# Hard attention in a four-layer graph kernel: a finished tile is added to X by ScalarE and GpSimd instead of VectorE

## What is computed

```python
attn = jnp.einsum('hqd,hkd->hqk', Q, K) * SCALING + energy
attn = attn + jnp.where(adj > 0, 0.0, -jnp.inf)
attn = jax.nn.softmax(attn, axis=-1)
hard = (attn == jnp.max(attn, axis=-1, keepdims=True)).astype(jnp.float32) / HEADS
out = jnp.einsum('hqk,hkd->hqd', hard, V)
return out.transpose(1, 0, 2).reshape(n, EMBED)
...
x = x + _L2_gnn_ref(h, adj, ...)
```

## Time and profile before

| what | value |
|---|---|
| median of 3 runs | 2402.12 us (2400.92 to 2402.3) |
| the profiled execution: its time / its span | 2401.43 / 2399.7 us |
| DVE busy, share of the span | 1979.6 us, 82% |
| PE busy / PEld busy | 2103.3 / 1713.7 us |
| ACT busy / POOL busy | 1768.2 / 694.6 us |
| hard attention, first DVE chunk to last X addition | 1331.0 to 2162.1 us |
| granted TensorE clock, mean | 0.949 of full speed |

### The profile page before, as it was taken

How to read it: one execution, slowest core, us unless ns; L and a number is a source line. 1 busy time by engine, 2 the same in 40 slices (tenths; PEclk the granted TensorE clock), 3 DMA queues, 4 the chain that set the end, 5 groups by cost and what they waited for, 6 DMA issues and landing times. The chain is left out here.

```text
span 2399.7 us, 62590 instructions
## 1 busy us (share of the span) xinstructions
PE 2103.3 (88%) x25316; PEld 1713.7 (71%) x25316; DVE 1979.6 (82%) x4384; ACT 1768.2 (74%) x2206; POOL 694.6 (29%) x646
## 2 busy tenths in 40 slices
PE   4647999999957999999978798999998999884999
PEld 3537999999944888888855466666666666554888
DVE  5566999999985988888867799999999999995122
ACT  4546999999975877777754688888888988884000
POOL 0020000000000000000003677778777877860000
PEclk9958999999978999999979799999999999996999
DMA  9787212212102011101007211111111111202222
GB/s 298 278 322 300 91 62 72 81 60 88 58 5 71 22 43 43 43 22 43 23 14 171 93 65 65 66 65 65 65 65 52 50 62 65 65 5 77 71 75 68
DMA packets 78474, 201.08 MB, mean 84 GB/s; under 512 B 26897, under 2 KB 44491, under 8 KB 74745
## 3 DMA queue, kind: packets, MB, share of 16 engines
q1 hardware_dynamic: 77432, 197.27, 24.5%
q10 hardware_dynamic: 768, 0.00, 0.0%
HBM read 161.87 MB, written 26.86 MB: 79 GB/s over the span
## 5 line engine op out<-in xcount | busy, mean ns | idle before, releaser
L1614 DVE CUSTOM_DVE_ANT_0 h_S<-h_ps,h_off 128x832 f32<-128x832 f32 x832 | 800.4, 1019 | 13.9 <-POOL h_off L1476 10.8
L1521 PE MATMUL h_ps<-KS,h_QS 98*128 98x416 f16 x1664 | 442.2, 348 | 99.9 <-DVE h_mx L1614 65.6
L1581 ACT ACTIVATE h_H<-h_S,h_nmx 128x2048 fp8e4<-128x2048 f32 x208 | 416.6, 2003 | 110.5 <-DVE h_nmx L1620 110.5
L834 ACT ACTIVATE b_CA<-b_el,HC 128x1152 fp8e4<-128x1152 f32 (+1 forms) x384 | 435.4, 1219 | 3.2 <-DMA b_el<-el_dram 3.2
L931 PE MATMUL b_pb<-b_x,b_B 128*128 128x132 f16 x5408 | 414.2, 221 | 3.9 <-DVE b_B L896 3.4
L931 PEld LDWEIGHTS b_pb<-b_x,b_B 128*128 128x128 fp8e4 x5408 | 340.3, 96 | 6.6 <-DVE b_B L896 6.2
L1482 POOL TENSOR_SCALAR h_gap<-h_S,h_nmx 128x1280 f32<-128x1280 f32 x208 | 277.1, 1332 | 145.0 <-DVE h_nmx L1620 142.5
L912 PE MATMUL b_pz<-b_x,adjT 128*128 128x134 f16 x2704 | 256.5, 221 | 15.8 <-DMA b_x<-xv_dram 15.8
L1487 POOL TENSOR_SCALAR h_H<-h_gap 128x1280 uint8<-128x1280 f32 x208 | 260.5, 1252 | 17.1
L1552 PEld LDWEIGHTS h_po<-Vhl,h_HT 128*128 128x128 fp8e4 x5408 | 214.8, 98 | 65.0 <-ACT h_HT L1588 0.7
L1245 PE MATMUL c_pd<-c_mv,WnT 128*128 128x256 f16 x2028 | 250.9, 275 | 10.8 <-DMA c_ad<-adjT_dram 10.8
(11 more groups left out here) (208 smaller groups left out, 3300.5 us busy)
## 6 DMA issues: line engine op xcount, KB each, us to landing
h_rows<-in_adj_dram SPq DMA_DIRECT2D x25, 1663.5 KB, 7.7
b_x<-xv_dram SPq DMA_DIRECT2D x48, 435.5 KB, 5.2
s_rows<-in_adj_dram SPq DMA_DIRECT2D x25, 832.0 KB, 6.7
s_rows<-in_adj_dram SPq DMA_DIRECT2D x25, 831.5 KB, 8.1
adjT_dram<-adjT SPq DMA_DIRECT2D x1, 10816.0 KB, 38.0
c_ad<-adjT_dram SPq DMA_DIRECT2D x13, 832.0 KB, 6.1
m_ad<-adjT_dram SPq DMA_DIRECT2D x13, 832.0 KB, 4.5
b_el<-el_dram SPq DMA_DIRECT2D x16, 576.0 KB, 3.8
```

The costliest lines, as they stand in the source:

```text
L834: nc.scalar.activation(dst[:, 0:cols], elr[:, n % 2, 0:cols], ACT.Sigmoid, bias=HC[:, h, 1, jt:jt + 1], scale=STEP, saturate=False).then_i ...
L1521: last = nc.tensor.matmul(ps[:, ch % 2, b, 0:SB], QS[:, i % 2, h, :], KS[:, h, c0:c0 + SB], start=True, stop=True)
L1581: nc.scalar.activation(H[:, g % 2, 0:CA], S[:, g % 2, 0:CA], ACT.Exp, bias=nmx[:, g % 2:g % 2 + 1], scale=1.0, saturate=False).then_inc(s_ ...
L1614: nc.vector.tensor_tensor_reduce(out=two(S[:, g % 2, ch * SW:(ch + 1) * SW]), in0=ps[:, ch % 2, :, 0:SB], in1=two(off[:, i % 2, ch * SW:(c ...
```

## The change

The two VectorE instructions of `result` go. In their place ScalarE copies the whole PSUM bank of a tile, scaled, into a new SBUF buffer `R` (`take_result`), and GpSimd adds the high half and then the low half of R to X (`add_result`, two instructions). ScalarE's copy stands at the end of head 3 of the following tile, GpSimd's additions after `not_hot` of heads 4 and 5. `R` exists once; the copy waits for the additions of the tile before.

GpSimd's mask parts move: until now two in head 0 and one in each of heads 1 to 5 and 7, now two each in heads 7, 0, 1 and 2, and none in heads 3 to 6. PE's wait for a free `po` bank is now on ScalarE's copy. The query load on SP now waits for the scores of the tile that used the buffer, where it waited for that tile's result.

```diff
-OFF_AT = [(1, (1, 2)), (1, (3,)), (1, (4,)), (1, (5,)), (1, (6,)), (1, (7,)), (1, ()), (2, (0,))]
-RESULT_AT = 3
+OFF_AT = [(1, (2, 3)), (1, (4, 5)), (1, (6, 7)), (1, ()), (1, ()), (1, ()), (1, ()), (2, (0, 1))]
+RESULT_AT, ADD_AT = 3, 4
...
+        R = k.sb(c, "h2_R", [P, HEADS, 2, HD], F32)
...
                 if i >= 2:
-                    sp.wait_ge(s_x, i - 1)
+                    sp.wait_ge(s_sc, SCH * HEADS * (i - 1))
                 sp.dma_start(QS[0:3 * HD, i % 2], q_dram[:, :, i * P:(i + 1) * P]).then_inc(s_q[i % 2], 16)
...
+            def add_result(i, part):
+                if part == 0:
+                    pool.wait_ge(s_res, i + 1)
+                else:
+                    pool.wait_ge(s_x, 2 * i + 1)
+                xs = k.X[:, i, :].rearrange("p (h d) -> p h d", d=HD)
+                nc.gpsimd.tensor_tensor(xs, xs, R[:, :, part, :], ALU.add).then_inc(s_x, 1)
...
             offsets(1, 0)
+            offsets(1, 1)
             for g in range(G):
...
+                if i and h in (ADD_AT, ADD_AT + 1):
+                    add_result(i - 1, h - ADD_AT)
                 j, parts = OFF_AT[h]
...
+            add_result(NT - 1, 0)
+            add_result(NT - 1, 1)
...
                     if h == 0 and i >= 2:
-                        pe.wait_ge(s_x, i - 1)
+                        pe.wait_ge(s_res, i - 1)
...
+            def take_result(i):
+                act.wait_ge(s_av, (i + 1) * HEADS)
+                if i:
+                    act.wait_ge(s_x, 2 * i)
+                nc.scalar.activation(R[:].rearrange("p h a d -> p (h a d)"), po[:, i % 2, :], ACT.Copy,
+                                     scale=1.0 / QKSC).then_inc(s_res, 1)
+
             for g in range(G):
                 weights(g)
                 if g >= 1:
                     evacuate(g - 1)
+                if g % HEADS == RESULT_AT and g > HEADS:
+                    take_result(g // HEADS - 1)
             evacuate(G - 1)
+            take_result(NT - 1)
...
-            def result(i):
-                dve.wait_ge(s_av, (i + 1) * HEADS)
-                xs = k.X[:, i, :].rearrange("p (h d) -> p h d", d=HD)
-                both = po[:, i % 2, :].rearrange("p (h a d) -> p h a d", a=2, d=HD)
-                nc.vector.scalar_tensor_tensor(xs, both[:, :, 0, :], 1.0 / QKSC, xs, ALU.mult, ALU.add).then_inc(s_r, 1)
-                dve.wait_ge(s_r, i + 1)
-                nc.vector.scalar_tensor_tensor(xs, both[:, :, 1, :], 1.0 / QKSC, xs, ALU.mult, ALU.add).then_inc(s_x, 1)
```

More of the change, by code:

```diff
@@ L1424, in hard_attend @@
     nc = k.nc
-    s_pad, s_nb, s_sc, s_tt, s_mx, s_hA, s_gap, s_hB, s_trA, s_trB, s_evA, s_evB, s_av, s_x, s_r, s_be = (
-        k.sem(f"s_h2_{n}") for n in ("pad", "nb", "sc", "tt", "mx", "hA", "gap", "hB", "trA", "trB", "evA", "evB", "av", "x", "r", "be"))
+    s_pad, s_nb, s_sc, s_tt, s_mx, s_hA, s_gap, s_hB, s_trA, s_trB, s_evA, s_evB, s_av, s_x, s_res, s_be = (
+        k.sem(f"s_h2_{n}") for n in ("pad", "nb", "sc", "tt", "mx", "hA", "gap", "hB", "trA", "trB", "evA", "evB", "av", "x", "res", "be"))
     s_rows = [k.sem(f"s_h2_rows{i}") for i in range(2)]
@@ L1497, in _ @@
                 if i == NT - 3 and h == 0:
-                    pool.wait_ge(s_nb, OFF_PARTS * (NT - 2) + 1)
+                    pool.wait_ge(s_nb, OFF_PARTS * (NT - 2) + 2)
                     pool.wait_ge(s_hB, g + 1)
@@ L1636, in _ @@
                 maximum(g)
-                if g % HEADS == RESULT_AT and g > HEADS:
-                    result(g // HEADS - 1)
-            result(NT - 1)
 def layer2(k, ap):
```

## The result

The changed kernel takes 2383.55 us (median of 4 runs, 2383.03 to 2383.85); the kernel before, run beside it, 2402.21 us. The ratio is 0.9922 with a 95% interval of [0.9906, 0.9938], 18.7 us or 0.8% faster. The forecast was 2383.3.

The account below looks back on a forecast made before the run. VectorE was taken to bound the hard attention. From the profiled 2401.43 us, -20.0 + 0 + 0.45 + 1.1 = -18.45 gave 2383.0; the forecast median was 2383.3, range 2380 to 2391.

Parts of the forecast that it names:

- What goes: Results of tiles 0 to 24 leave VectorE's list in the loop: 25 x 0.80 = 20.0 us saved.
- ScalarE's copy: One 597 ns copy a tile, absorbed by ScalarE's pause and PE's slack: 0 us, at most 9.0.
- GpSimd's additions in the loop: Two additions a tile after heads 4 and 5, 0.60 us each, within GpSimd's pause: 0 us.
- the tolerance: How late GpSimd may be before VectorE loses time: about 2.0 us, read from tile 23.
- The lateness that the mask parts build up: GpSimd loses 0.15 us in each of heads 7, 0, 1 and 2, 0.60 in all, at no cost.
- Tile 23: Behind GpSimd's clearing, heads with two mask parts can't win time back: 0.15 us three times, +0.45.
- The end: The last tile's copy and two additions, covered by nothing: +1.1 us, or +3.2 with the upper addition price.
- The queues: SP's query loads are issued some heads sooner, but loads were hidden already: 0 us.
- Rival 1: GpSimd's additions shut VectorE out at SBUF, holding up a chunk of maxima each: 2413 us, 4 in 100.
- Rival 2: ScalarE's copy isn't absorbed by its pauses and PE's slack: 2392 us at the bound, 13 in 100.
- rival 3: Another engine takes VectorE's place, the beat stretches and nothing is gained: 2401 to 2403 us, 2 in 100.

Follow-up runs that it names:

- e1: The kernel before with only GpSimd's mask parts moved, VectorE still adding the results: 2403.62 us, ratio 1.0002 to the kernel before.
- e3: The changed kernel with ScalarE making the copy of a finished tile three times in tiles 0 to 24: 2404.12 us, ratio 1.0011 to the kernel before.
- e5: The changed kernel with one spare addition before each of GpSimd's additions in tiles 0 to 24: 2382.03 us, ratio 0.9915 to the kernel before.
- e2: The changed kernel with the mask parts left where they were before: 2385.25 us, ratio 0.9929 to the kernel before.
- e4: The changed kernel with both additions from R on VectorE, after the maximum of head 4: 2487.82 us, ratio 1.035 to the kernel before.

## Why the prediction was right, step by step

- **What goes: -20.0 forecast, -19.75 measured.** 25 beats fell by 0.79. That nothing else stretched is the core of the forecast, and e1 shows that moving the mask parts has no share in the gain.
- **ScalarE's copy: 0 forecast, 0 measured.** 597 ns as priced, and 0.04 us late where I had 0.08 to 0.23. That it could have cost something is shown by e3: three copies cost 20 us. Of the slack I named the wrong wait: in e3 0.63 of the 0.81 us a tile is VectorE's chunk 0 behind the exponential, which the prediction doesn't have among the waits.
- **GpSimd's additions in the loop: 0 forecast, 0 measured.** Their size was off: 0.60 taken, 0.73 measured, between my bounds of 0.50 and 1.67. With the tolerance it makes no difference, nor would twice the additions (e5). The lateness that the mask parts build up was right, 0.64 against 0.60.
- **Tile 23: +0.45 forecast, +0.51 measured,** and the three beats show the mechanism as told, 0.16, 0.17 and 0.18. But that the clock held behind the stop was luck: it fell there in three of nine traces, for 0.4 to 1.1 us more (e1, e2). I had priced a stop of PE by its own length alone.
- **The end: +1.1 forecast, +1.33 measured.** The mis-sized term is the addition, 2 x 0.13 us.
- **The queues: 0.** VectorE's stop at the start is 11.0 us where it was 10.8, and no beat of the loop shows a wait for them. No run tests this term by itself.
- **The rivals.** Rival 1 would have needed VectorE's chunks to be held up; e5 excludes it, and e4 shows the very mechanism on the instruction that has two SBUF inputs. Rival 2 is excluded by the unchanged beat, rival 3 by the same. Against rival 3 the prediction has 1.18 us of idle time on GpSimd "in each" plain head; that row is of the last tile, which makes no masks, and with one mask part the idle time was 0.56 (at 2063.37 in tile 23), which still was enough. The rule of the Trainium skill, page "GPSIMD Engine Reference", section 4.1 Engine selection, put an addition at an estimated 0.84 us by twice VectorE's 0.42; it is 0.73. Here it doesn't decide: with the additions on VectorE, as the rule has them, the kernel before is 18.7 us slower, and e4, which has them there from SBUF, 104.

The sum was -18.45 against -18.0 between the profiled spans; the result, the end and tile 23 each came out a little worse than forecast, 0.5 in all, and what lies ahead of the stage and behind it (+0.61 and -0.31), the first tile and the single beats (-0.36) nearly cancel out. That the forecast met the median within 0.3 us is luck, since terms that it didn't have are as large; that it met it within a microsecond or two is not.

## What to carry to other kernels

VectorE was full without a stop here, and 0.80 us moved off it paid although it became 2.06 us on two other engines (0.60 + 2 x 0.73), because these have a pause in each period and a buffer's distance to whoever waits for them. To judge such a move, price the pause, the tolerance (a place where the engine was already late shows it), and the last period, where nothing is hidden. Look at where an instruction's inputs lie before choosing its engine: the same addition took VectorE 0.42 us alone and 1.35 beside GpSimd's reads, and cost nothing when GpSimd did it in its pause. A stop of PE costs more than its length when the granted clock falls behind it (0.4 us more in e1, 1.1 in e2).

## What the runs showed of the hardware that I had not expected

- A VectorE addition of 128x256 with both inputs in SBUF sat out whole GpSimd instructions that read SBUF: 1354 ns median against 425 ns alone, each ending 0.27 to 0.28 us behind the GpSimd instruction (e4). VectorE's chunks with one input in PSUM and one in SBUF didn't notice GpSimd's two-input additions at all, 1019 ns (e5).
- The granted clock was 0.57 over the 4 us behind a rest of PE's weight loads of 2.03 us in e2, and 1.00 behind rests of 2.03 us (before), 2.19 (changed) and 2.39 (e5) at the same place. What decides between them the runs don't show.
- GpSimd's addition of 128x256 from SBUF takes 729 ns and follows h_H without a gap (1510.63 against 1510.66), where mask parts start 0.08 behind it.
